# Encoder attention on one core: the products with the values issued for two groups at a time instead of for one

## The reference, cut to what matters

```python
for l in range(L):                                   # L = 4
    y = _layer_norm(h, ln_a[l, 0], ln_b[l, 0])
    qkv = jnp.einsum('bsd,tde->tbse', y, attn_w[l, :3]) + attn_b[l, :3][:, None, None, :]
    q, k, v = [t.reshape(b, s, H, DK).transpose(0, 2, 1, 3) for t in qkv]   # H = 16, DK = 16
    scores = jnp.einsum('bhqd,bhkd->bhqk', q, k) * inv_sqrt_dk
    p = jax.nn.softmax(scores, axis=-1)
    o = jnp.einsum('bhqk,bhkd->bhqd', p, v).transpose(0, 2, 1, 3).reshape(b, s, D)
    h = h + o @ attn_w[l, 3] + attn_b[l, 3]
    y = _layer_norm(h, ln_a[l, 1], ln_b[l, 1])
    h = h + jax.nn.relu(y @ w1[l] + b1[l]) @ w2[l] + b2[l]
```

## Time and profile before

| | us |
|---|---|
| median of 3 runs | 2078.26 (2077.49 to 2080.31) |
| the profiled execution, its own time | 2074.87 |
| its span | 2072.9 |
| TensorE matmul busy | 2013.2 (97%) |
| TensorE weight load busy | 1659.8 (80%) |
| VectorE busy | 1299.1 (63%) |
| ScalarE busy | 1039.5 (50%) |

### The profile page before, as it was taken

One profiled execution on the slowest core, in us unless ns is written; L12 is line 12 of the kernel. 1 busy time (PEld: TensorE's weight loads), 2 busy tenths in 40 slices (PEclk: granted clock), 3 DMA queues, 4 the chain that ended last, 5 costly groups with the idle time before them and its releaser, 6 DMA issues. The chain is left out here.

```text
span 2072.9 us, 42265 instructions
## 1 busy us (share of the span) xinstructions
PE 2013.2 (97%) x16462; PEld 1659.8 (80%) x16462; DVE 1299.1 (63%) x3344; ACT 1039.5 (50%) x3525; POOL 215.8 (10%) x251
## 2 busy tenths in 40 slices
PE   5999999999999999999999998999999999999998
PEld 4788888888888888888888877788878788877776
DVE  5776776677676767767767753677776546422332
ACT  4666666666566665666666651554454531111111
POOL 4000000000000000000000000000000000334444
PEclk9999999999999999999999999999999999999999
DMA  5000000100000400000000001300000100025542
GB/s 185 2 2 1 2 2 2 70 2 1 2 2 1 157 2 2 1 2 2 1 2 1 2 2 40 146 1 1 1 1 1 62 1 11 28 85 159 168 134 64
DMA packets 27203, 69.84 MB, mean 34 GB/s; under 512 B 9920, under 2 KB 17825, under 8 KB 23680
## 3 DMA queue, kind: packets, MB, share of 16 engines
q1 hardware_dynamic: 18432, 59.42, 8.5%
q0 software_dynamic: 6400, 5.63, 1.1%
q10 hardware_dynamic: 2176, 2.10, 0.3%
HBM read 61.16 MB, written 17.40 MB: 38 GB/s over the span
## 5 line engine op out<-in xcount | busy, mean ns | idle before, releaser
L547 ACT ACTIVATE probs<-bank,nmax 128x256 f32<-128x256 f32 x1024 | 469.4, 481 | 230.3 <-DVE nmax L712 230.3
L712 DVE TENSOR_REDUCE nmax<-bank 128x2 f32<-128x512 f32 x512 | 322.1, 681 | 78.0 <-PE bank L402 78.0
L415 PE MATMUL bank<-ident,probs 128*128 128x128 f32 x2048 | 281.6, 278 | 12.6 <-DVE pts L720 6.9
L415 PEld LDWEIGHTS bank<-ident,probs 128*128 128x128 f32 x2048 | 230.1, 141 | 59.8 <-issue 25.8
L556 ACT ACTIVATE pts<-bank 128x512 f32<-128x512 f32 x256 | 157.1, 614 | 173.1 <-PE bank L415 171.5
L447 PE MATMUL bank<-yT,weights 128*128 128x256 f32 x1024 | 237.9, 381 | 0.9 <-ACT aT L570 0.9
L459 PE MATMUL bank<-weights,aT 128*128 128x256 f32 x1024 | 231.6, 379 | 0.2 <-ACT rT L562 0.2
L547 ACT ACTIVATION_READ_ACCUMULATOR probs<-bank,nmax 128x1 f32 x1024 | 218.0, 213 | 0.0
L720 DVE COPY pts<-bank 128x512 f32<-128x512 f32 x256 | 175.6, 686 | 59.0 <-PE bank L415 55.3
L459 PEld LDWEIGHTS bank<-weights,aT 128*128 128x128 f32 x1024 | 191.9, 190 | 25.8 <-issue 0.6
L447 PEld LDWEIGHTS bank<-yT,weights 128*128 128x128 f32 x1024 | 188.1, 191 | 23.2 <-ACT aT L570 1.3
(11 more groups left out here) (218 smaller groups left out, 2933.7 us busy)
## 6 DMA issues: line engine op xcount, KB each, us to landing
wqkv<-in_experts SPq DMA_DIRECT2D x16, 1024.0 KB, 5.0
weights<-in_wtok SPq DMA_DIRECT2D x4, 2048.0 KB, 10.4
wqkv<-in_experts SPq DMA_DIRECT2D x16, 512.0 KB, 3.7
expert_rows<-xT_all SPq DMA_DIRECT2D x10, 546.0 KB, 16.5
xrows<-expert_rows SPq DMA_DIRECT2D x16, 273.0 KB, 3.2
weights<-in_wtok SPq DMA_DIRECT2D x3, 1024.0 KB, 4.7
wqkv<-in_wqkv SPq DMA_DIRECT2D x1, 3072.0 KB, 17.9
weights<-in_shared SPq DMA_DIRECT2D x1, 3072.0 KB, 12.0
```

Of the source, the lines that this page charges most:

```text
L415: last = pe.transpose(g[:, (NT * x + kb) * P:(NT * x + kb + 1) * P], p[:, x, kb * P:(kb + 1) * P], ident[:])
L547: last = nc.scalar.activation(probs[u % 8][:, x, :], g[:, x * S:(x + 1) * S], ACT.Exp, bias=nmax[j % 2][:, col:col + 1], accum_out=rsum[j ...
L712: nc.vector.tensor_reduce(nmax[j % 2][:, col:col + 2], g[:].rearrange("p (x s) -> p x s", x=2), AX.X, ALU.max, negate=True).then_inc(s_max, 1)
```

## The change

Slots with odd c issue `pv` for two groups in one piece, those three and two slots back; slots with even c issue none.

```diff
@@ -486,9 +486,10 @@
                 for c in range(GROUPS):
 
                     jp, cp = divmod(GROUPS * j + c - 1, GROUPS)
-                    jq, cq = divmod(GROUPS * j + c - 2, GROUPS)
                     scores(j, c)
-                    pv(jq, cq)
+                    if c % 2:
+                        for G in (GROUPS * j + c - 3, GROUPS * j + c - 2):
+                            pv(*divmod(G, GROUPS))
                     turn_probs(jp, cp, 0)
                     turn_probs(jp, cp, 1)
```

## The result

| | before | changed |
|---|---|---|
| median, us (4 runs each) | 2077.88 (2075.25 to 2080.31) | 2101.15 (2098.05 to 2103.52) |
| profiled execution, its own time | 2074.87 | 2098.05 |
| its span | 2072.9 | 2096.0 |

The ratio is 1.0111, 95% interval 1.0096 to 1.0127. The two profiled executions differ by 23.2 us; the sum said 24.7.

The account below looks back on a forecast made before the run. TensorE was taken to bound slot c = 0, a 7.5 us chain through other engines slot c = 2. Terms -3.9 + 1.7 + 26.1 + 0 + 0.9 - 0.1 = +24.7 us on 2078.26 gave 2103.0 us, range 2097 to 2112.

Parts of the forecast that it names:

- point 6: Start and end of the encoder: job 0 zero, job 1 +0.9 us for its c = 3, after the last scores -0.1 us.
- 1 and 2: TensorE's list: an even slot without pv is 1.01 us shorter, an odd slot with a second pv 0.87 us longer.
- 3: Slot c = 0 is shortened, ffn_down keeping 0.22 us margin: -3.9 us over 28 jobs, +1.7 us for jobs 29 and 30.
- 4: Slot c = 2 stays 9.84 us, its wait growing from 0.2 to 1.2 us; c = 3 pays 0.87 per job, +26.1 us.
- the chain: Slot c = 2: scores, row maximum, exponentials, y_out, copy_pt n = 1, turn_probs n = 3; claimed to set the slot, 7.5 us long.
- 5: Slot c = 1: VectorE stands 0.3 us for the later pv, delaying the last exponentials as much; counted as zero.
- A: Rival: both even slots, c = 0 and c = 2, take the saving; -8.2 us, time 2070.1 us; chance 4%.
- B: Rival: slot c = 0 loses its saving too as ffn_down waits; at worst +28 us on top, 2131 us; chance 7%.
- C: Rival: the odd slots had slack and absorb the pv; time near 2075 to 2078 us; chance 3%.
- rule on changes of tiling: Changing the tiling mode drains TensorE; by that alone, fewer changes make the kernel faster, 0.14 us per change fewer in a pair.

Follow-up runs that it names:

- late_max: Changed kernel with an unused second row maximum on VectorE ahead of the first in every slot c = 0; median 2112.82 us, ratio to before 1.0168.
- pair23: Kernel before with products paired only in slots c = 2 and 3 (none in c = 2, two groups in c = 3); median 2101.27 us, ratio 1.0121.
- the two short chains: Kernel before and changed kernel, each with most of the second normalisation and its y_out left out (result not computed); medians 2067.65 and 2060.50 us.
- the swap: ScalarE's copy_pt n = 1 put ahead of y_out in slot c = 2, in the changed kernel (2087.26 us) and in the kernel before (2071.32 us).
- pair01: Kernel before with products paired only in slots c = 0 and 1 (none in c = 0, two groups in c = 1); median 2072.02 us, ratio 0.9984.

## Why the prediction was right

The direction, the place and the mechanism came out as forecast. The time did too, but that its first and last parts add up to so little is in part luck (point 6). Point by point, from the profiles:

1 and 2, *what leaves an even slot and what an odd one gains*: 1.01 and 0.87 were forecast, and slots c = 0 and c = 1 moved by -1.01 and +0.87.

3, *slot c = 0 takes the saving*: it does, with 0.23 us of margin by late_max (0.22 was forecast; the release was put down to the wrong one of two instructions, without harm to the margin). In job 29 the slot kept its 9.80 us, with the whole saving turned into a wait:

```profile
1143.32 1.15 PE L402 MATMUL bank<-kT,qm 32*128 32x256 f32 x16
...
1148.18 3.69 PE L459 MATMUL bank<-weights,aT 128*128 128x256 f32 x16 [0.97 <-ACT probs L548]
...
1153.11 1.15 PE L402 MATMUL bank<-kT,qm 32*128 32x256 f32 x16
```

4, *slot c = 2 does not*: 9.84 us before and after, and the wait for the copy went from 0.2 to 1.2 us a job. pair23 shows that this pair alone makes the loss, the two short chains that the chain is its cause, and the swap that the order of ScalarE's list is a part of that chain. The "second normalisation" by which the prediction reads job 29 is that of the windowed attention (L97), not the encoder's `normalise(2, j - 1)`.

5, *added waits*: oT waited 0.35 us a job (0.3 forecast), at no cost to slot c = 1.

6, *the ends*: here the sum was off. Heads of jobs 2 and 28 of the changed kernel:

```profile
90.67 1.15 PE L402 MATMUL bank<-kT,qm 32*128 32x256 f32 x16
...
1103.33 1.15 PE L402 MATMUL bank<-kT,qm 32*128 32x256 f32 x16
```

| stretch | forecast | measured |
|---|---|---|
| up to job 2 | +0.9 | -0.5 (90.67 - 91.18) |
| jobs 2 to 27 | +19.1 (26 x 0.735) | +19.3 (1012.66 - 993.38) |
| job 28 to the last scores | +4.1 | +4.7 (152.24 - 147.50) |
| from there to the end | +0.7 | -0.3 (840.47 - 840.80) |
| sum (rows rounded) | +24.7 | +23.2 |

The granted clock, which no term of the sum has, is in all three rows that are off.

- *Up to job 2.* The +0.9 of job 1's slot c = 3 is there (9.17 to 10.04 us). But before spent 18.59 us in slots c = 0 and 1 of job 1, at a granted clock of 0.82, where the changed kernel spent 15.20 at 1.00; and the changed kernel was 2.0 us later at the head of job 1. The last section has more on this.
- *Job 28 to the last scores.* The 0.6 too much is slot c = 2 of job 31, counted as unchanged, which went from 11.64 to 12.28 us. It is in its last block, `ffn_up`, which ran partly at the lower clock level (1.2 GHz) in before (0.59 of full speed from 1228.25 to 1232.06 us) and wholly in the changed kernel (0.50 from 1251.11 to 1255.57); in both, TensorE had waited three times in that slot ahead of it, for 0.8 to 1.8 us each. Before, then changed:

```profile
1229.15 2.98 PE L447 MATMUL bank<-yT,weights 128*128 128x256 f32 x8
```

```profile
1252.02 3.62 PE L447 MATMUL bank<-yT,weights 128*128 128x256 f32 x8
```

- *From there to the end.* By the end of the encoder the changed kernel is 0.9 to 1.2 us further behind, near the forecast, and it stays so for 400 us. Then one block of the mixture of experts runs at the lower level in before (0.50 from 1651.20 to 1654.60 us) and at the full one in the changed kernel (1.00 from 1675.60 to 1678.00), behind the same wait of 2.60 us, and gives 1.5 us back. Before, then changed:

```profile
1651.54 3.49 PE L1212 MATMUL w_bank<-xT_all,weights 128*128 128x256 f32 x8 [2.60 <-DVE weights L1593]
```

```profile
1676.20 1.99 PE L1213 MATMUL w_bank<-xT_all,weights 128*128 128x256 f32 x8 [2.60 <-DVE weights L1594]
```

The change does not touch that block. These three rows came to +3.9 in all, where +5.7 was forecast, with misses of both signs that partly cancel, which is luck. The term that carries the forecast is the 26 jobs in the middle, and there the sum is right within 0.2 us. Why the clock fell where it did was not tried.

Of the rivals, A as the result is excluded by the unchanged slot c = 2, B by the 8.59 of slot c = 0, C by the 10.48 and 10.04 of the odd slots. The Trainium skill's rule on changes of tiling ("TensorEngine Tiling (Array Packing)", Key Properties) is borne out as a price: one change fewer is worth 0.14 us a pair, in pair01 and in the changed kernel's c = 0 and 1. Whether that price is a drain no run here shows, and it was overruled by where the other pair stands.

## What to carry to other kernels

Moving a block of work off one slot of a software pipeline and onto another costs nothing only if both slots are bound by the engine that does it. Where a slot is as long as a chain through the other engines that begins in it, taking work out of it saves nothing (here 1.01 us of it), and the work costs its full price where it goes (0.87). The sign of such a slot is small: here it was a single wait of 0.2 us a job on an engine that was 97% busy. So compare the end of the chain with the engine's arrival, and shorten the chain (here by two lines of ScalarE's list in another order) before taking work away.

## What the runs showed of the hardware beyond that

A change of tiling cost the same to whatever stood behind it: from scores to pv 1.07 us, from scores straight to transposes 1.07 or 1.08 in the even slots of the changed kernel. A second pv behind the first cost 0.87 although its weights and its data are another group's.

The start-up differed more than the forecast allowed, partly with the granted clock. Windows on slots c = 0 and 1 of job 1, before:

```profile
53.59:72.18 18.59, 16.12 (x153) 12.45 (x152) 11.84 (x29) 10.50 (x38) 0.72 (x1) 0.82 0.01 2
```

and in pair23, whose lists in these two slots are those of before:

```profile
53.85:69.17 15.32, 12.80 (x154) 10.35 (x153) 11.85 (x29) 10.49 (x38) 0.72 (x1) 1.00 0.01 2
```

So 3.3 us go with the clock, 0.82 of full speed against 1.00, and not with the list. In the first 3.70 us of job 1 it was 0.54 before, mostly the 1.2 GHz level, and the scores took 1.92 us to the next block; at 2.4 GHz, in the changed kernel, they took 1.08. In before TensorE had idled 1.09 and 1.22 us in the slot ahead. But such waits do not decide it alone: pair01, whose list up to there is that of before, idled as long, and its clock was 1.00 over the scores that followed, from 54.86 us. TensorE in that slot of pair01:

```profile
52.39 0.66 PE L415 MATMUL bank<-ident,probs 128*128 128x128 f32 x4 [1.09 <-DVE pts L723]
54.27 0.66 PE L415 MATMUL bank<-ident,probs 128*128 128x128 f32 x4 [1.23 <-ACT pts L559]
```

Over the ten traces of this study job 2 began anywhere from 84.4 to 92.8 us, with edits that hardly touch the first jobs. What of this is the clock and what is the first loads was not tried; it is some us that no per-slot sum will find.
